# Row scatters of the second MoE layer: a count of attention scores added before each of the first 32

## The reference, cut to what matters

```python
x = x + 0.5 * moe(layernorm(x))      # 16 experts, each token to its top 4
x = x + attention(layernorm(x))      # 16 heads of 16 features, causal, ALiBi bias
x = x + 0.5 * moe(layernorm(x))

# attention
scores = einsum('bhid,bhjd->bhij', q, k) * scale + alibi_causal_bias(s, 16)
out = einsum('bhij,bhjd->bhid', softmax(scores), v)
return out @ Wo + bo

# moe
vals, idx = top_k(t @ gate_w.T + gate_b, 4)
delta = sum of the 4 chosen experts' outputs, weighted by softmax(vals)
```

## Time and profile before

| | us |
|---|---|
| median of 3 runs | 1021.15 (1018.97 to 1021.18) |
| the profiled execution | 1019.23 |
| its span, first to last instruction | 1017.5 |
| PE, PEld busy | 722.9, 428.6 |
| DVE, ACT, POOL busy | 610.9, 445.6, 328.3 |

### The profile page before, as it was taken

The page is one execution under the profiler, slowest core; times in us unless marked ns, Lnnn a source line. Parts: engine busy times, 40 slices in busy tenths (PEclk is TensorE's granted clock), DMA queues, the critical chain, the costliest instruction groups (busy, mean ns, idle before and its releaser), DMA issues.

```text
span 1017.5 us, 22304 instructions
## 1 busy us (share of the span) xinstructions
PE 722.9 (71%) x5722; PEld 428.6 (42%) x5722; DVE 610.9 (60%) x1961; ACT 445.6 (44%) x974; POOL 328.3 (32%) x356
## 2 busy tenths in 40 slices
PE   2222079999899917778889488487129999999930
PEld 2111046666565613223343243244116666666620
DVE  6778235666555564787787368347305666665647
ACT  2534035555555524357465235261015555555510
POOL 3667713333333314101111600605512333333320
PEclk9999999999999966889999788797559999999975
DMA  9754345555444253631201313315333333333148
GB/s 311 261 212 161 136 118 167 168 168 169 131 136 127 76 176 93 197 116 49 80 18 53 132 45 130 131 44 202 118 106 99 98 99 101 95 96 91 50 133 280
DMA packets 120111, 131.63 MB, mean 129 GB/s; under 512 B 39596, under 2 KB 101525, under 8 KB 119864
## 3 DMA queue, kind: packets, MB, share of 16 engines
q1 hardware_dynamic: 101656, 91.11, 29.9%
q0 software_dynamic: 13728, 34.64, 9.5%
q10 hardware_dynamic: 4608, 4.46, 1.2%
HBM read 69.54 MB, written 64.21 MB: 131 GB/s over the span
## 4 chain that ended last, share of the span: by engine, by line
PE 44%; SPq 14%; DVE 13%; issue 13%; ACT 5%; another core or an unknown queue 5%; ACTq 3%; DMA 3%; DVEq 0%; POOLq 0%; POOL 0%
PE banks L407 13%; PE banks L429 6%; SPq L218 3%; ACT w2s L1434 3%; SPq L232 3%; SPq L217 2%; PE banks L1211 2%; PE banks L1165 2%; DVE X L727 2%; SPq L230 2%; PE banks L1277 2%; PE banks L1235 2%; PE banks L403 2%; PE banks L416 2%
## 5 line engine op out<-in xcount | busy, mean ns | idle before, releaser
L341 POOL DMA_INDIRECT y_rows<-y,goal x158 | 155.6, 985 | 318.5 <-ACT y L499 296.0
L407 PE MATMUL banks<-w1s,rT 128*128 x948 | 233.7, 383 | 0.0
L689 DVE TENSOR_SCALAR pbh<-banks 128x256 f32<-128x256 f32 x158 | 67.1, 425 | 197.3 <-ACT pbh L485 125.9
L1597 DVE CUSTOM_DVE_ANT_0 pbh<-banks,maskq 128x128 bf16<-128x128 f32 (+3 forms) x256 | 114.0, 487 | 77.8 <-PE banks L1188 46.3
L1434 ACT ACTIVATE w2s<-banks 128x1024 f32<-128x1024 f32 (+3 forms) x128 | 89.7, 701 | 123.4 <-PE banks L1219 84.3
L407 PEld LDWEIGHTS banks<-w1s,rT 128*128 128x128 f16 x948 | 93.7, 99 | 97.2 <-issue 4.0
L429 PE MATMUL banks<-w2s,hsT 128*128 x948 | 129.2, 273 | 0.0
L478 ACT ACTIVATE rT<-banks 128x512 f16<-128x512 f16 x158 | 93.5, 593 | 42.7 <-issue 34.7
L485 ACT ACTIVATE pbh<-banks 128x256 f32<-128x256 f32 x158 | 60.5, 383 | 117.3 <-PE banks L407 113.9
L1125 POOL DMA_INDIRECT x_rows<-row,row_to x64 | 61.7, 964 | 121.8 <-DVE row_to L1731 103.5
L389 PE MATMUL banks<-ident,row 128*128 128x128 f16 x632 | 62.6, 223 | 51.2 <-DMA goal<-x_rows 50.4
(11 more groups left out here) (238 smaller groups left out, 1059.7 us busy)
## 6 DMA issues: line engine op xcount, KB each, us to landing
row<-x_rows SPq DMA_DIRECT2D x158, 128.0 KB
arena<-in_w SPq DMA_DIRECT2D x16, 512.0 KB, 7.1
w1s<-y_rows SPq DMA_DIRECT2D x16, 512.0 KB, 4.7
arena<-y_rows SPq DMA_DIRECT2D x16, 512.0 KB, 7.8
qk_split<-w1s SPq DMA_DIRECT2D x48, 128.0 KB
arena<-qk_split SPq DMA_DIRECT2D x64, 96.0 KB, 2.3
w_lent<-w1s SPq DMA_DIRECT2D x22, 256.0 KB
w1s<-w_lent SPq DMA_DIRECT2D x11, 512.0 KB
```

Source lines behind the costliest of these rows:

```text
L341: pool.indirect_dma_start(y_rows[m], bass.IndirectOffsetOnAxis(ap=goal[:, n % NG, :], axis=0), y[:, n % NY, :], None, bounds_check=K * T - ...
L407: mm = pe.matmul(o, rT[:, n % 2, 2 * r + k, :], w1s[:, bass.ds(e, 1), k, w, :], start=False, stop=(k == HC - 1 and w == 1))
L689: dve.tensor_scalar(b[:, n % 2, :], bank[2 + n % 2][:, INNER:], (LIMIT + 1.0) * S, (1.0 - LIMIT) * S, ALU.min, ALU.max).then_inc(each("b"), 1)
L1597: dve.tensor_tensor_reduce(junk[:, (n * U + j) % 3, 0:W], query_bank[(n * U + j) % 3][:, 0:W], maskq[:, SEQ - W:], 1.0, -3e38, ALU.add, AL ...
```

## The change

Before each of the 16 scatters of batch 0 and of the 16 of batch 1, POOL additionally waits for a count of `scores_k`. With j = 0 to 15 the number of the scatter in its batch, batch 0 waits for 74 + 2j (from unit 9 to the end of unit 12, one scatter for every two steps), and batch 1 for 105 + 3j // 2 (unit 13 to the seventh step of unit 15, two scatters for every three steps). The loops that issue the scatters are written as one; their order among POOL's instructions is the same as before.

```diff
                     pool.wait_ge(route("row_hi"), NT + i + 1)
                     pool.wait_ge(route("row_to"), B + i // TPB + 1)
                     for k in range(K):
+                        j = i % TPB * K + k
+                        if i // TPB == 0:
+                            pool.wait_ge(s("scores_k"), 9 * KS + 2 * j + 2)
+                        if i // TPB == 1:
+                            pool.wait_ge(s("scores_k"), 13 * KS + j * 3 // 2 + 1)
                         pool.indirect_dma_start(x_rows[1], bass.IndirectOffsetOnAxis(ap=row_to[:, i, k:k + 1], axis=0),
                                                 row[:, i % NR, :], None).then_inc(scattered[i % NR], 16)
@@
                     if n % 4 == 3 and n // 4 + 2 < B:
                         add_bo(n // 4 + 2)
-                    if n >= 9:
-                        scatter(n - 9)
-                for i in range(PERIODS - 9, NT):
+                for i in range(NT):
                     scatter(i)
```

## The result

| | before | after |
|---|---|---|
| median of the runs, us | 1021.16 (1018.97 to 1022.03, 4 runs) | 990.55 (986.59 to 994.41, 4 runs) |
| profiled execution; its span | 1019.23; 1017.5 | 990.5; 988.8 |
| seven units 9 to 15, to the last exponential | 127.0 | 98.1 |
| from the last exponential to the span's end | 331.2 | 330.0 |

The last two rows are from the profiled executions, in us. The ratio is 0.9704, with a 95% interval of 0.9673 to 0.9734. The forecast was 996, the range 985 to 1009.

The account below looks back on a forecast made before the run. The attention was taken as bound by the loop score, exponential, score, held up by dense scatters in units 9 and 13. 1019.2 - 33.3 + 9.9 = 995.8 us, predicted as 996, range 985 to 1009.

Parts of the forecast that it names:

- The mechanism: Attention units 9 and 13: dense scatters make TensorE's reports reach ScalarE and VectorE about 4.5 us late.
- The gain of 33.3 us: Removing the dense streams gives back 18.15 us in unit 9 and 15.1 in unit 13; 32.0 to 34.6 together.
- The price of 9.9 us: Cost of 32 scatters spread over units 9 to 15: 8.7 us for 29, 1.2 for three; ends 0 and 18.3.
- half of the upper end: Price of each spread scatter in units 9 to 15: 0.3 us, from an upper end of 0.59 us.
- The three in a row: Batch 1's first three scatters in unit 13 go almost as densely as before, charged 1.2 us.
- The forecast's 23.4: Net saving in the attention: the 33.3 us gain less the 9.9 us price.
- The tail: Last projection, batch 2's first scatter and second MoE layer after the attention all start earlier by the same 23 us.
- The waits themselves: POOL's added waits in the attention: later ends of batches 0 and 1 are hidden, with 20 us of cover.
- Batch 1's pitch is too dense: Rival, units 13 to 15: pairs break the loop, only batch 0's gain stays; 1006 to 1009 us; chance 0.07.
- A scatter costs the same wherever it is: Rival, units 9 to 15: 1.04 us per scatter wherever placed, time stays 1019 to 1021 us; chance 0.06.
- Slower: Rival, units 9 to 15: each single scatter delays TensorE's reports; at 1.5 us each, 1034 us; chance 0.06.
- The scatters aren't the cause: Rival, units 9 and 13: ranking and locating hold the loop, or streams stay dense; 1019 to 1021 us; chance 0.03.

Follow-up runs that it names:

- y1_streams: Changed kernel plus 16 64-byte-row scatters (unit 1), 16 full-row scatters (unit 5), 16 plain DMAs (unit 7), batch 0 in eights; 1037.42 us, before 1021.95.
- e1_batch0_only: Changed kernel without batch 1's added waits, batch 0's scatters still spread; 964.95 us, beside 972.44 for the kernel before.
- z1_best: Changed kernel with batch 1 waiting in pairs and batch 2's last 7 scatters held for batch 3's mask; 1003.2 us, before 1029.24, ratio 0.9753.

## Why the prediction was right, and what was mis-sized

**The mechanism** held in what the change rests on: dense scatters make the stall, and room between them removes it. "TensorE's report of finished work reaches the two others about 4.5 us late while scatters follow one another without a pause" was called a reading and not yet proven. y1_streams shows the cause: scatters put into a unit that had none bring the stall with them, 17 us for 16, and ScalarE starts 5.0 and 12.6 us after the matmuls that it waits for. Whether the report leaves TensorE late or is noticed late is still a reading. For the first speaks that ScalarE's and VectorE's waits end together; for something wider speaks that ScalarE's own queue is slowed in the tail.

**The gain of 33.3 us** was right to 0.5. Unit 9 was put at 15.35 us clean; with four scatters in it, it takes 15.48, and 15.47 on the chip without the stall. Unit 13 was put at 13.0; clean it is 13.34 (e1_batch0_only). That is 33.53 - 15.47 + 28.04 - 13.34 = 32.8 us. Both sizes were middles of two or three neighbours that lie 1.7 and 0.9 us apart, so part of that closeness is luck.

**The price of 9.9 us** is the term that was mis-sized. In the prediction's terms it measured 4.3: 2.2 in unit 13, 0.1 in unit 9, and 2.0 in the other five units together (65.46 us before, 67.44 after). The step that failed is "I take 0.3 us, half of the upper end". That upper end came from two scatters at the dense pitch, at the head of a run, and from a step of unit 1 (1.44 us), where the same step of unit 13 takes 1.66 us without the stall. It is no price of a scatter that stands alone: units 10, 11 and 14, with 13 scatters, are 0.3 us longer in all. Not even all of the 2.0 us need be the scatters': on chip 7 the same five units are 0.75 us longer, and units 12 and 15 differ by up to 1.4 us between runs in which nothing stalls. The nearer row was the one of the second MoE layer, which had said nothing. The three in a row that were charged 1.2 us are four, and cost about 2.

**The check by the whole**: 33.25 - 4.3 = 28.9 us in units 9 to 15. Unit 9 starts 1.4 us later than before (560.67 against 559.3, ahead of any edit), and the tail is 1.2 us shorter, which gives 28.7, the difference of the spans. The forecast's 23.4 is 5.3 less: 5.6 from the price, less the 0.2 of these two shifts. Two smaller slips: the sum of 995.8 us is one of profiled executions, and the 1.9 us by which these lay under the median were not added; and the runs of the kernel after spread by 0.8% (986.59 to 994.41 us), where the prediction counted on 0.3%.

**The tail** moved as a block, as predicted: batch 2's first scatter from 695.39 to 667.53, 27.9 us earlier. On chip 7 it did so less well, giving 2.5 us back; one profile of each doesn't tell whether that is the change or the spread of the tail. **The waits themselves** cost nothing that shows, and POOL was free when `row_to` of batch 2 came (7.66 us idle).

**The rivals.** "Batch 1's pitch is too dense" is out as priced: in unit 14 the pairs at 637.25 and 642.88 leave it at 13.36 us. A little of it is true, by place: in z1_best the pairs in unit 14 cost 1.7 us. "A scatter costs the same wherever it is" is out: single ones are free, the sixteenth of a run costs a microsecond. "Slower" is out with it. "The scatters aren't the cause" is out on chips 5 and 7. The Trainium skill's rule ("SBUF — State Buffer", section "Who interferes with whom"), that only the shared port pair contends and that TensorE and ScalarE never wait on anyone, matches chips 2 and 11, where 16 dense scatters leave unit 5 at 16.18 us and unit 13 at 13.34. On chip 5 the trace disagrees with what the prediction drew from it: 33.4 us. The compute instructions themselves aren't slowed there either (ScalarE is busy for 6.55 us in unit 5, 6.59 before), so this is no contention in the work; what waits is the passing on of finished work, which the rule doesn't speak of.

**What the prediction didn't see** is that all of it holds only on some chips, or at some times. The runs that the result rests on, and chips 5, 7 and 14, show before at 1021 to 1031 us; chips 2 and 11 show 964 and 972. On those the range would have been missed on the good side and the change would have been called no change. That the result was measured where the stall exists is luck. Nothing in one profile could have told this.

## What to carry to other kernels

When two engines that wait for different results of a third are released in the same moment, and the profile names no instruction as the releaser, look at what a fourth one issues meanwhile. A dense run of indirect DMAs from POOL is worth breaking up where a tight loop between engines stands beside it: one or two at a time are nearly free, four cost 2 to 3 us, sixteen 17. But delay only those with slack behind them: z1_best held back scatters on the way to the end, and its last stream ended 6.5 us later. And time such a change on more than one chip before the gain is given a size.

## What the runs showed of the hardware that was not expected

- **The stall is there on some chips and not on others** (or at some times; the two weren't separated). With the stall (the runs of the result, chips 5, 7, 14) before takes 1021 to 1031 us, without it (chips 2, 11) 964 to 972. Of the 54 us between the profiled spans (1017.5 against 963.2 in e1_batch0_only) 32 are in units 9 to 15, 11 in the tail (331 against 320 us) and about 10 ahead of the first exponential (427 against 416 to 419 us); the fast side is read from changed kernels, since the kernel before has no profile there. Scatters stand in all three parts. That those in the other two are the cause there too was not tried.
- **The cost goes with the length of the run.** Two scatters in a row cost up to some 0.6 us (three pairs in unit 14 of z1_best cost 1.7), four (with a pair behind them) some 2 to 3.5, eight 7.2 and 8.0, sixteen 15 to 18; after the last scatter has started, 3 to 4 us pass until the loop goes on (530.42 to 533.39 in y1_streams).
- **Rows of 64 bytes do as much as rows of 1088**: 16 to 18 us in units 1 and 2 against 17.2 in unit 5. Sixteen plain DMAs of POOL with as many packets and bytes as the latter cost nothing.
- **ScalarE's own DMA issuing is held up as well**: 16 writes of padding take 26.5 us beside a stream of 16 scatters, 36.0 beside one of 23, and 18.8 on a chip without the stall. In the first case its pieces go in steps of 0.70 us. A little of this shows on the chip without the stall as well: one of its register loads takes 0.51 to 0.53 us beside the scatters in e1_batch0_only, and 0.29 us in the kernel after once the stream is over.
- **A stall costs TensorE its clock besides.** In unit 9 it was busy for 18.04 us at a granted clock of 0.75 and is now for 13.32 at 1.00, the same 135 matmuls; in y1_streams unit 5, where it is busy for half of the time, has 0.69. 1.00 is the upper of the two levels, 2.4 GHz, and a mean below it has a part at 1.2 GHz in it.
